# Maxima transposed into the bank of the value sums, and the first bf16 term of queries and keys rounded straight from PSUM

## The reference

```
mod = (silu(c) @ wmod).reshape(4, 6, 1, 256)          # sa, ca, ga, sb, cb, gb
h   = layernorm(x) * (1 + ca) + sa
q, k, v = split(h @ qkv_w + qkv_b)                    # 16 heads of 16
scores  = q k^T / 4, for 0 <= i - j < 128             # local window
local   = softmax(scores) v
rq      = h @ rq_w + rq_b                             # 4 latent heads of 16
rk, rv  = split(mean over 16 tokens of h @ rkv_w + rkv_b)
remote  = softmax(rq rk^T / 4, earlier chunks) rv @ rout_w + rout_b
gate    = sigmoid(local @ gl_w + remote @ gr_w)
x = x + ga * ((gate * local + (1 - gate) * remote) @ out_w + out_b)
h = layernorm(x) * (1 + cb) + sb
x = x + gb * (layernorm(2 h) * ln_g + ln_b)
```

## Time and profile before

| | |
|---|---|
| median of 3 runs | 576.77 us (572.23 to 577.25) |
| profiled execution | 576.64 us, of which 574.9 us is the span from the first to the last instruction |
| mean granted clock of TensorE | 0.949 of full speed |
| busy, share of the span | PE 482.9 us (84%), DVE 436.6 (76%), POOL 379.2 (66%), PE weight loads 364.1 (63%), ACT 353.8 (62%) |
| chain of work that ended last | PE 72%, issue 11%, POOL 5%, DVE 4%, DMA 2%, ACT 2% |

### The profile page before, as it was taken

How to read it: one execution, slowest core, us unless ns; L and a number is a source line. 1 busy time by engine, 2 the same in 40 slices (tenths; PEclk the granted TensorE clock), 3 DMA queues, 4 the chain that set the end, 5 groups by cost and what they waited for, 6 DMA issues and landing times.

```text
span 574.9 us, 19855 instructions
## 1 busy us (share of the span) xinstructions
PE 482.9 (84%) x7168; PEld 364.1 (63%) x7168; DVE 436.6 (76%) x1193; ACT 353.8 (62%) x868; POOL 379.2 (66%) x516
## 2 busy tenths in 40 slices
PE   2446689999899999999999999999999999988771
PEld 2205567777677666777777676777776676766451
DVE  2155657788688888988988788888888887878554
ACT  1210466677677667777777577777776776766540
POOL 2222346778577767788877587777777677766663
PEclk9975889999899999999999899999999999999776
DMA  9558644618244444434252607162534444440000
GB/s 277 114 133 246 163 105 99 132 47 187 56 113 75 95 94 93 94 90 93 64 101 68 119 34 145 39 125 62 120 68 97 92 94 93 82 79 10 11 10 19
DMA packets 56523, 55.15 MB, mean 96 GB/s; under 512 B 7380, under 2 KB 53100, under 8 KB 54892
## 3 DMA queue, kind: packets, MB, share of 16 engines
q1 hardware_dynamic: 53564, 52.57, 41.4%
q10 hardware_dynamic: 2864, 1.31, 1.1%
HBM read 37.07 MB, written 16.80 MB: 94 GB/s over the span
## 4 chain that ended last, share of the span: by engine, by line
PE 72%; issue 11%; POOL 5%; DVE 4%; DMA 2%; ACT 2%; ACTq 1%; SPq 1%; POOLq 0%; DVEq 0%
PE p_pv L819 9%; PE p_qkv L730 9%; PE p_qkv L740 6%; PE p_misc L886 6%; PE p_y L806 5%; PE p_x L785 5%; PE p_y L807 5%; PE p_x L778 4%; PE p_a L751 3%; PE p_qkv L860 3%; PE p_misc L869 2%; PE p_a L831 2%; PE p_a L716 2%; PE p_misc L877 2%; PE p_a L753 2%
## 5 line engine op out<-in xcount | busy, mean ns | idle before, releaser
L592 ACT ACTIVATE pr<-p_y 128x512 f32<-128x512 f32 x224 | 124.6, 595 | 55.8 <-PE p_y L807 52.9
L1159 DVE TENSOR_REDUCE mtok<-p_x 128x3 bf16<-128x480 f32 (+1 forms) x192 | 109.3, 585 | 30.9 <-PE p_x L785 29.6
L441 POOL TENSOR_SCALAR_AFFINE_SELECT pr<-pr 128x512 f32<-128x512 f32 x128 | 89.6, 701 | 11.2 <-ACT pr L594 9.0
L451 POOL TENSOR_TENSOR rstd<-ve,half 128x1 f32<-128x1 f32 x96 | 58.1, 605 | 47.9 <-DVE ve L1079 47.7
L469 POOL TENSOR_TENSOR dif<-local,rem 128x272 f32<-128x272 f32 x32 | 30.9, 965 | 83.8 <-DVE local L1197 83.8
L445 POOL TENSOR_SCALAR_AFFINE_SELECT pr<-pr 128x512 f32<-128x512 f32 x112 | 81.3, 726 | 0.0
L807 PE MATMUL p_y<-qst,kst 112*128 112x128 bf16 x512 | 73.2, 221 | 0.0
L806 PE MATMUL p_y<-qst,kst 112*128 112x128 bf16 x448 | 66.5, 221 | 7.7 <-ACT pr L592 4.8
L819 PE MATMUL p_pv<-pr,vp 128*18 128x128 f32 x1920 | 67.1, 279 | 2.1 <-POOL pr L445 0.8
L730 PE MATMUL p_qkv<-hT,wqk 128*128 128x256 f32 x256 | 66.1, 403 | 2.2 <-DVE qkf L1111 1.3
L740 PE MATMUL p_qkv<-wv,hT 128*128 128x272 f32 x128 | 40.1, 439 | 29.5 <-issue 29.4
(11 more groups left out here) (131 smaller groups left out, 1092.7 us busy)
## 6 DMA issues: line engine op xcount, KB each, us to landing
scr_q<-terms SPq DMA_DIRECT2D x16, 384.0 KB, 2.5
qst<-scr_q SPq DMA_DIRECT2D x16, 384.0 KB, 4.7
scr_k<-terms SPq DMA_DIRECT2D x16, 384.0 KB, 4.4
kst<-scr_k SPq DMA_DIRECT2D x16, 384.0 KB, 5.4
qst<-scr_q SPq DMA_DIRECT2D x16, 256.0 KB, 5.4
kst<-scr_k SPq DMA_DIRECT2D x16, 256.0 KB, 6.4
out_y<-y SPq DMA_DIRECT2D x32, 128.0 KB, 1.7
x_all<-in_x SPq DMA_DIRECT2D x3, 1024.0 KB, 8.3
```

What stands on the lines that cost most here:

```text
L441: ins = pool.affine_select(out=own, in_=own, compare_op=ALU.is_ge, fill=0.0, base=-1, pattern=[[0, 4], [1, P]], channel_multiplier=-1)
L592: act.activation(pr[:, 2 * i:2 * i + 2, :, :], src, ACT.Exp).then_inc(exp_done[i], 1)
L1159: dve.tensor_reduce(mtok[:, KS + h0:KS + h1], p_x[i % 2][:, 0:(h1 - h0) * w].rearrange("p (h n) -> p h n", n=w), AX_X, ALU.max, negate=Tru ...
```

## The change

Two things are changed, and both take a user away from a place where another one waits. First, `max_t` transposes into p_pv. It must then wait until `out_t` of the tile before has copied the value sums out of p_pv. Its place on PE is behind the first group of `scores`; mtok gets two buffers; `project_v` waits for `remote` of an older tile in place of `shift`, and `lat_remote` no longer names `shift`. Second, `part1` reads p_qkv itself and adds the bias in the pass: two ACT passes of 128x256 with a per-partition bias, in place of one 128x512 from qkf. It now runs one slot function earlier, for tile t + 3, between `exps` 4 and 7. DVE's `residual` takes the place of `copy_qk` and of POOL's `res1`: PSUM plus bias minus the first term, two passes of 128x256. In the setup the calls for the first three tiles follow the same way.

```diff
             def part1(t):
                 half = t % 2
+                act.wait_ge(qk_psum, done(t))
+                act.wait_ge(terms_stored[half], halves(t - 2, 16))
+                for b in range(KC):
+                    ins = act.activation(term(half, 0)[:, b, :], p_qkv[:, 2 * b * P:2 * (b + 1) * P], ACT.Identity,
+                                         bias=bqk[:, half, b:b + 1])
+                ins.then_inc(part1_ready, 1)
...
             def part2(t):
                 half = t % 2
                 act.wait_ge(qk_copied, done(t))
-                act.wait_ge(terms_stored[half], halves(t - 2, 16))
-                act.activation(term(half, 0), qkf[:, half, :, :], ACT.Copy).then_inc(part1_ready, 1)
...
-                act.wait_ge(res_ready, done(t))
...
             def project_v(t):
                 pe.wait_ge(hT_ready, done(t))
-                pe.wait_ge(shift_ready, done(t - 2))
+                pe.wait_ge(rem_ready, done(t - 3))
                 pe.wait_ge(qk_copied, done(t + 1))
...
             def max_t(t):
                 pe.wait_ge(s_max[LAST_MAX], done(t))
-                pe.wait_ge(qk_copied, done(t + 3))
-                pe.wait_ge(rem_ready, done(t - 1))
-                pe.transpose(p_qkv[:, 0:P // 2].bitcast(BF16), mtok[:, :], ident_bf[:, :]).then_inc(mT_psum, 1)
+                pe.wait_ge(oT_ready, done(t - 1))
+                pe.transpose(p_pv[:, 0:P // 2].bitcast(BF16), mtok[:, t % 2, :], ident_bf[:, :]).then_inc(mT_psum, 1)
...
-            def copy_qk(t):
+            def residual(t):
                 half = t % 2
-                dve.wait_ge(qk_psum, done(t))
+                dve.wait_ge(part1_ready, done(t))
                 dve.wait_ge(part3_ready, done(t - 2))
-                dve.tensor_tensor(qkf[:, half, :, :], p_qkv[:, :].rearrange("p (b n) -> p b n", b=KC),
-                                  bc(bqk[:, half, :], 2 * P), ALU.add).then_inc(qk_copied, 1)
+                for b in range(KC):
+                    ins = dve.scalar_tensor_tensor(out=qkf[:, half, b, :], in0=p_qkv[:, 2 * b * P:2 * (b + 1) * P],
+                                                   scalar=bqk[:, half, b:b + 1], in1=term(half, 0)[:, b, :],
+                                                   op0=ALU.add, op1=ALU.subtract)
+                ins.then_inc(qk_copied, 1)
```

More of the change, by code:

```diff
@@ L139, in build @@
         bvd = sb("bvd", [P, 2, 2, P])
-        mtok = sb("mtok", [P, P], BF16)
+        mtok = sb("mtok", [P, 2, P], BF16)
         pr = sb("pr", [P, H, 2, P])
@@ L211, in build @@
                                                       counted("rvb_ready", "DVE"), counted("bvd_ready", "DVE"))
-        part1_ready, res_ready = counted("part1_ready", "ACT"), counted("res_ready", "POOL")
+        part1_ready = counted("part1_ready", "ACT")
         part2_ready, part3_ready = counted("part2_ready", "ACT"), counted("part3_ready", "POOL")
@@ L419, in scale_weights @@
                 pool.tensor_scalar(wrv[:, :, :], wrv[:, :, :], 1.0 / CH, None, ALU.mult).then_inc(su_pool, 1)
-            def res1(t):
-                pool.wait_ge(part1_ready, done(t))
-                half = t % 2
-                pool.tensor_tensor(qkf[:, half, :, :], qkf[:, half, :, :], term(half, 0), ALU.subtract)\
-                    .then_inc(res_ready, 1)
             def part3(t):
@@ L488, in slot @@
                 A, Q, T, C, D = ("A" in stages, "Q" in stages, "T" in stages, "C" in stages, "D" in stages)
-                if Q:
-                    res1(r)
                 if A:
@@ L516, in _ @@
             scale_weights()
-            res1(b0)
             rstd1(b2)
             part3(b0)
-            res1(b1)
             part3(b1)
@@ L582, in shift @@
                 act.wait_ge(st_psum[LAST_ST], done(t - 4))
-                act.activation(q_of(t)[KS:KS + H, :, :], p_qkv[KS:KS + H, 0:P // 2].bitcast(BF16).unsqueeze(1).to_broadcast([H, H, P]),
+                act.activation(q_of(t)[KS:KS + H, :, :], p_pv[KS:KS + H, 0:P // 2].bitcast(BF16).unsqueeze(1).to_broadcast([H, H, P]),
                                ACT.Copy).then_inc(shift_ready, 1)
@@ L640, in slot @@
             def slot(t, stages):
-                a, r, m, c = t + LEAD, t + 2, t - 1, t - 2
-                A, Q, S, T, C = ("A" in stages, "Q" in stages, "S" in stages, "T" in stages, "C" in stages)
-                if Q:
-                    part1(r)
+                a, h, r, m, c = t + LEAD, t + 3, t + 2, t - 1, t - 2
+                A, PR, Q, S, T, C = ("A" in stages, "P" in stages, "Q" in stages, "S" in stages, "T" in stages, "C" in stages)
                 if C:
@@ L667, in slot @@
                     exps(m, 4)
+                if PR:
+                    part1(h)
+                if T:
                     exps(m, 7)
@@ L680, in _ @@
             part1(b0)
+            part1(b1)
             part2(b0)
             modulated(b2)
-            part1(b1)
             part2(b1)
             modulated(b3_)
+            part1(b2)
             run(slot)
@@ L858, in lat_remote @@
                 pe.wait_ge(v_copied, done(t + 2))
-                pe.wait_ge(shift_ready, done(t))
                 pe.matmul(p_qkv[:, 0:D + H], loT[:, :], wro[:, :, :].rearrange("p h k -> p (h k)"), start=True, stop=True).then_inc(rem_psum, 1)
@@ L893, in slot @@
                 A, PR, K, S, T, C = ("A" in stages, "P" in stages, "K" in stages, "S" in stages, "T" in stages, "C" in stages)
+                if S:
+                    scores(t, 1)
                 if T:
@@ L896, in slot @@
                 if S:
-                    scores(t, 1)
                     scores(t, 0)
@@ L1155, in maxima @@
                 dve.wait_ge(s_psum[i], done(t))
-                dve.wait_ge(mT_psum, done(t - 1))
+                dve.wait_ge(mT_psum, done(t - 2))
                 h0, h1 = S_HEADS[i]
                 w = WIN if t % NB else P
-                dve.tensor_reduce(mtok[:, KS + h0:KS + h1], p_x[i % 2][:, 0:(h1 - h0) * w].rearrange("p (h n) -> p h n", n=w),
+                dve.tensor_reduce(mtok[:, t % 2, KS + h0:KS + h1], p_x[i % 2][:, 0:(h1 - h0) * w].rearrange("p (h n) -> p h n", n=w),
                                   AX_X, ALU.max, negate=True).then_inc(s_max[i], 1)
@@ L1316, in slot @@
                 if PR:
-                    copy_qk(h)
+                    residual(h)
                 if S:
@@ L1335, in _ @@
             dve.wait_ge(su_act, SA_QK)
-            copy_qk(b0)
+            residual(b0)
             dve.wait_ge(loaded_x1, 16)
@@ L1340, in _ @@
             add_eps1(b2)
-            copy_qk(b1)
+            residual(b1)
             norm1(b2)
@@ L1355, in _ @@
             spread_rv(b0)
-            copy_qk(b2)
+            residual(b2)
             dve.wait_ge(loaded_g, 16)
```

2 lines of the change are left out of this document (1 added, 1 removed).

## The result

The changed kernel takes 584.23 us (median of 4 runs, 580.03 to 586.26) against 576.35 for the kernel before, run beside it: a ratio of 1.016, 95% interval 1.0106 to 1.0214. It is slower by 1.6%, where 573 was forecast. The profiled execution is the slowest of the four, 586.26; its span is 584.5 against 574.9. Ratios here count only executions within 1.5% of their kernel's fastest, which leaves out some of the kernel before and five of run 7's ten (the others have a median of 569.3), so a ratio need not be the quotient of the medians beside it.

A forecast was written before the change was run, and what follows sets the result against it. A slot was bounded by 3.24 us (out_t, part2, shift) plus 12.03 of PE work from project_v on. Gains of 4.2 and 0.45 less 0.5 and 0.7, net 3.4, took 576.64 to 573.2, rounded to 573; range 567 to 580.

The forecast's parts named there:

- The slots behind the short ones: Slots following t = 1, 9, 17, 25: each shares the short slot's loss; 0.5 us off for three of them.
- the like slots: Fourteen slots like slot 19 (or near it) gain 0.30 us each, 4.2; nine like slot 21 gain 0.05, 0.45.
- start and end: Start: about 1.0 us later, given back by slot 1; slots 30 to 32: 0.7 lost as PE waits for shift.
- The bound, and the release of project_v: PE's 1.26 us wait for shift ahead of project_v in slot 19 goes; a 0.53 wait at max_t replaces it.
- Up to the projections: Slot 19, us after slot start: project_v at +2.33, project_half at +8.2 instead of +9.09, 0.9 early.
- Part1: On ACT ahead of exps 7: two passes stepping 0.74 us (bounds 0.56 and 0.92), so exps 7 starts at +10.94.
- rival (a): Part1's pass is hidden in ACT's 1.14 us idle ahead of exps 7, not delaying it: 561 us, chance 0.10.
- What follows exps 7: Everything in sequence: 1.02 us to mixT, then 2.95 to the slot's end; slot 19 gains 0.36.
- rival (b): Nothing is left of the gain in the slots, with part1 stepping its upper bound, 0.92 us: 577 us, chance 0.20.
- DVE came out as said: Residual's two passes on DVE take 0.8 to 0.9 us, 0.2 more than the former one: no gain, no loss.
- The DMA chain: Key terms stored, then loaded for the next slot's first scores: timing kept, +14.6; slots 1, 9, 17, 25 gain nothing.
- rival (c): Slower: k stack at +16.1 holds scores 1, max_t and shift; 0.65 us lost in 15 slots, 583 us, chance 0.10.

The follow-up runs named there:

- run 7: Changed kernel with SP's query-stack load ahead of the output store in even slots, part2 ahead of out_t, and part3 ahead of rstd1: 572.38 us, ratio 0.9874.
- run 3: Changed kernel with max_t ahead of scores 1 on PE in the four slots behind the short ones (t = 2, 10, 18, 26): 579.82 us, ratio 1.0098.
- run 6: Changed kernel with SP issuing the query-stack load ahead of the output store in even slots: 575.13 us, ratio 1.002.
- run 1: Kernel before with only max_t in p_pv behind scores 1, two mtok buffers and project_v freed from shift (bank half): 573.51 us, ratio 0.9966.
- run 5: Changed kernel with part1 back at the end of ACT's slot and residual behind finish on DVE: 568.79 us, ratio 0.9858.
- run 2: Changed kernel with max_t back in p_qkv, first in the slot, and project_v waiting for shift (terms half alone): 588.0 us, ratio 1.0223.

## Why the prediction was wrong

Against a net gain of 3.4 the profiled run lost 9.6, a miss of 13.0. The slots behind the short ones make 12.9 of it (+12.48, where the sum had a gain of 0.4: three at 0.30, less 0.5), the like slots 4.0; the short slots took back 3.3 that were not forecast, of which 1.5 is luck of the run before (its slot 17), and start and end came out 0.5 better.

**The bound, and the release of project_v.** The view of what bounds the kernel was right: project_v waits for nothing (L734 above), and max_t has the foreseen wait, 0.52 against 0.53. Slot 19 of the changed kernel, which starts at 353.10 - 0.13 = 352.97 (as 345.20 stands to 345.33 in the earlier trace rows), on PE, ACT and POOL:

```profile
352.85 0.27 PE L772 MATMUL p_x<-edge,ident_bf 128*32 128x192 bf16 x4
...
353.85 0.22 PE L788 MATMUL p_pv<-ident_bf,mtok 128*128 128x128 bf16 x1 [0.52 <-ACT oT L592]
...
355.44 1.18 PE L734 MATMUL p_qkv<-wv,hT 128*128 128x272 f32 x4
...
361.33 1.95 PE L724 MATMUL p_qkv<-hT,wqk 128*128 128x256 f32 x8
...
365.45 1.13 PE L878 MATMUL p_misc<-wo,mixT 128*128 128x256 f32 x4 [0.37 <-ACT mixT L630]
366.66 1.51 PE L812 MATMUL p_pv<-pr,vp 128*18 128x128 f32 x48
...
353.10 0.60 ACT L592 ACTIVATE oT<-p_pv 128x512 f32<-128x512 f32 x1 [2.66 <-PE p_pv L812]
...
363.32 0.84 ACT L561 ACTIVATE terms<-p_qkv,bqk 128x256 bf16<-128x256 f32 x2 [0.92 <-PE p_qkv L724]
364.05 1.08 ACT L584 ACTIVATE pr<-p_y 128x512 f32<-128x512 f32 x2
365.00 0.40 ACT L630 ACTIVATE mixT<-p_misc 128x256 f32<-128x256 f32 x1
...
365.20 0.63 POOL L434 TENSOR_SCALAR_AFFINE_SELECT pr<-pr 128x512 f32<-128x512 f32 x1 [0.50 <-ACT pr L584]
365.79 0.82 POOL L438 TENSOR_SCALAR_AFFINE_SELECT pr<-pr 128x512 f32<-128x512 f32 x1
```

**Up to the projections: mis-sized.** Project_v is at +2.47 (forecast +2.33) and project_half at +8.36 instead of +8.2: 0.73 early, not 0.9.

**Part1: right in price and place.** It starts at +10.35 with project_half's result, steps 363.32 to 364.05 = 0.73 (0.74 was forecast), and exps 7 follows at once: nothing hides it, and rival (a) is out. The Trainium skill (ScalarE: Activation LUTs, What ACT_TABLE_LOAD costs) would have a pass at 492 ns and the step at 0.80, an estimate from its figures; the trace has 470 ns (L561 above) and 0.73, a little less of each.

**What follows exps 7: a step left out.** The working went from the exponentials to mixT and on to the end at 2.95. The last value sums also wait for the masks that POOL lays on these very exponentials: POOL stood idle for 0.50 ahead of them, their last ends at 366.61, and the sums start at 366.66. No run tests this step by itself. From mixT to the end it is 3.10 (365.00 to 368.10, where the next slot starts by the same 0.13). So slot 19 gained 0.15 instead of 0.36. In slot 21, which starts at 383.40, project_half comes at +8.79, 0.30 early and not 0.48, and the sums wait for POOL:

```profile
392.19 1.95 PE L724 MATMUL p_qkv<-hT,wqk 128*128 128x256 f32 x8
...
397.63 1.51 PE L812 MATMUL p_pv<-pr,vp 128*18 128x128 f32 x48 [0.19 <-POOL pr L438]
```

It lost 0.29 where 0.05 was to be gained. These two steps put the like slots at +0.2 (-1.54 + 1.76) where -3.75 stood in the sum for these twenty (11 at 0.30, 9 at 0.05). That is the outcome of rival (b), nothing left, but not its reason, since part1 did not come to its upper bound. DVE came out as said, with residual at 0.47 a pass.

**The DMA chain: the step that failed.** "So the four slots t = 1, 9, 17, 25 gain nothing, and the slot behind each shares that loss", and 0.5 was taken off for it. Measured, slots 10, 18 and 26 cost 8.2 more than before, and slot 2, which the sum left out, 4.3. That the chain keeps its time was nearly right: the load of k was at +6.8 in slot 25 before and is at +6.6 in slot 17 now, the scores get the stack at +14.6 and +14.99. But the short slots did gain 0.63 (13.84 to 13.21), so the scores now wait 1.6 to 2.0 in place of 0.54 and 0.64. Before, such a wait cost nothing: shift ran beside it, and project_v waited for shift anyway (slots 10 and 26: 15.28, like their neighbours). That slack, 1.26 in slot 19, is what the change took away. Now the late scores hold project_v up themselves, and max_t and shift, which stand behind them, add a little (run 3). PE and ACT at the start of slot 18:

```profile
335.19 0.27 PE L772 MATMUL p_x<-edge,ident_bf 128*32 128x192 bf16 x4 [1.65 <-issue]
...
335.60 0.23 PE L788 MATMUL p_pv<-ident_bf,mtok 128*128 128x128 bf16 x1
...
335.87 1.87 ACT L575 ACTIVATE qst<-p_pv 16x2048 bf16<-16x2048 bf16 x1 [1.14 <-PE p_pv L788]
```

This is near rival (c), and its time of 583 is close to what was measured, but by luck: it put the price in the held-up shift, 0.65 in each of 15 slots with the stack at +16.1, and gave it a chance of 0.10. The stack came hardly later, and three of the slots had been shorter than the chain from the start: arrival at +14.6 behind a slot of 13.84 is 0.78 into the next slot, past the prediction's own 0.53, but the working set it against slots of 14.9.

**The clock, left out altogether.** Slot 10 shows the wait by itself: 16.54, 1.3 over before. Slots 18 and 26 lost 4.2 and 2.7, slot 2 4.3, and there TensorE's granted clock fell behind the wait. The stretches of slot 18, columns as above:

```profile
333.40:335.19 1.79, 0.15 (x8) 0.03 (x1) 1.05 (x5) 1.11 (x2) 0.56 (x2) 1.00 0.31 76
335.19:338.24 3.05, 3.05 (x54) 2.12 (x54) 1.66 (x4) 2.35 (x5) 2.48 (x3) 0.61 0.32 113
338.24:342.40 4.16, 4.16 (x32) 3.25 (x32) 1.86 (x8) 1.69 (x9) 0.00 (x0) 0.50 0.05 16
```

PE is busy for 0.15 of 1.79, then runs at 0.61 and 0.50 (1.2 GHz in place of 2.4) until behind 342.40. By the difference to slot 10 that is, as an estimate, 19.49 - 16.54 = 2.95 in slot 18 and 1.45 in slot 26. Run 6 shows that the late stack is behind wait and fall here: the load came 1.5 earlier, slots 10 and 18 were 15.13, and both stayed at full clock. But a wait does not always bring the fall: ahead of slots 10, 18 and 26 run 1 waited 1.50, 1.50 and 2.14 and run 5 0.56, 1.59 and 1.23, all at full clock. So what the falls add to the median of the changed kernel is not shown.

**The two halves.** Runs 1 and 2 divide the blame. The bank half alone comes out at 0.9966, since it shortens the short slots too and takes away the slack that hid the stack. The terms half alone is 2.2% slower, by part1 ahead of the exponentials. Together they keep both costs.

## What to carry to other kernels

A shorter stage shows the next fixed chain. Ahead of a change that shortens a slot, list the transfers that cross it with their time from issue to first use, and compare them with the shortest slot, not with the typical one. When a step is moved ahead of others on an engine, follow what it delays through every engine to the last consumer (here exponentials, masks, value sums), and look for a place at the end of the queue where the engine waits anyway: that place was worth 15 us between the medians here (run 5). And a transfer that is late may lie behind another one: moving the query load by 2.9 us (slot 17, run 6) gave what making the terms 2.5 us earlier could not. A wait that costs nothing today is hidden by something; before a change removes that, list the waits that it hides.
